# Probabilities and values of the last two units of self attention in fp32, weighted by single fp32 matmuls

## What is computed

```python
q = (x @ Wq.T + bq).reshape(B, T, N_HEADS, HEAD_DIM)
k = (x @ Wk.T + bk).reshape(B, T, N_KV_HEADS, HEAD_DIM)
v = (x @ Wv.T + bv).reshape(B, T, N_KV_HEADS, HEAD_DIM)
...
scores = jnp.einsum('bgkqd,bkld->bgkql', q, k) * SCALE
scores = jnp.where(causal, scores, jnp.float32(-jnp.inf))
w = jax.nn.softmax(scores, axis=-1)
out = jnp.einsum('bgkql,bkld->bgkqd', w, v)
```

## Time and profile before

| | |
|---|---|
| runs, us | 2606.54, 2605.93, 2609.09; median 2606.54 |
| profiled execution, us | 2608.02 |
| its span, us | 2606.2 |
| granted clock of TensorE, mean | 0.969 |
| busy: PE, DVE, ACT, POOL | 94%, 68%, 63%, 59% |

### The profile page before, as it was taken

How to read it: one execution, slowest core, us unless ns; L and a number is a source line. 1 busy time by engine, 2 the same in 40 slices (tenths; PEclk the granted TensorE clock), 3 DMA queues, 4 the chain that set the end, 5 groups by cost and what they waited for, 6 DMA issues and landing times.

```text
span 2606.2 us, 48453 instructions
## 1 busy us (share of the span) xinstructions
PE 2454.7 (94%) x17800; PEld 1350.7 (52%) x17800; DVE 1778.4 (68%) x2988; ACT 1638.7 (63%) x2998; POOL 1528.1 (59%) x1363
## 2 busy tenths in 40 slices
PE   7999999999986568999999999999999999999999
PEld 4667777777765453444444444444444444444444
DVE  6656777767777877777777777777777897645311
ACT  4556666666665447777777777777777786545100
POOL 2556677767778567777777777777766433212100
PEclk9999999999997679999999999999999999999999
DMA  6252433333322321222222222222223844323232
GB/s 218 89 160 89 125 123 121 113 107 102 92 86 82 96 73 41 89 90 89 86 85 86 86 84 91 89 90 92 87 84 106 262 138 150 107 90 106 70 109 76
DMA packets 224827, 271.09 MB, mean 104 GB/s; under 512 B 36560, under 2 KB 147664, under 8 KB 224592
## 3 DMA queue, kind: packets, MB, share of 16 engines
q1 hardware_dynamic: 224592, 268.00, 32.7%
HBM read 192.94 MB, written 73.40 MB: 102 GB/s over the span
## 4 chain that ended last, share of the span: by engine, by line
PE 54%; POOL 3%; issue 1%; DVE 1%; ACT 1%; DMA 0%; DVEq 0%; ACTq 0%; POOLq 0%
PE ps L2176 32%; PE ps L2209 22%; POOL q_rows L513 1%; POOL p L494 1%; POOL xn L2083 1%; POOL xT L483 0%; DMA h_parts<-xn 0%; DVE p L462 0%; DVE ps L462 0%; ACT q_rows L509 0%; POOL x_row L2089 0%; ACT w_l L452 0%; DVE xT L477 0%; ACT xn L2270 0%; ACT ps L449 0%
## 5 line engine op out<-in xcount | busy, mean ns | idle before, releaser
L462 DVE TENSOR_TENSOR ps<-ps,w_l 128x512 f32<-128x512 f32 x672 | 444.1, 693 | 242.8 <-ACT w_l L452 165.3
L1024 POOL TENSOR_TENSOR arena<-p,arena 128x512 f16<-128x512 f32 x320 | 370.8, 1167 | 227.6 <-ACT arena L1508 227.0
L483 POOL TENSOR_TENSOR xT<-xT,nat 128x512 f32<-128x512 f32 x162 | 206.4, 1274 | 451.9 <-DVE xT L477 451.9
L452 ACT ACTIVATE w_l<-proj 128x512 f32<-128x512 int32 x672 | 398.6, 617 | 60.9 <-DVE ps L462 51.7
L1500 ACT ACTIVATE p<-ps 128x512 f32<-128x512 f32 x320 | 191.1, 597 | 265.2 <-PE ps L1276 260.1
L1719 DVE TENSOR_REDUCE block_max<-ps 128x4 f32<-128x512 f32 x320 | 218.9, 687 | 176.0 <-PE ps L1247 173.4
L449 ACT ACTIVATE ps<-proj,small 128x512 f32<-128x512 int32 x336 | 217.7, 680 | 168.9 <-DVE xT L477 166.2
L2176 PE MATMUL ps<-arena,q_rows 128*128 128x512 f16 x1344 | 296.7, 380 | 5.4 <-DVE x_row L2356 3.8
L2436 DVE SCALAR_TENSOR_TENSOR arena<-ps,arena 128x1024 f32<-128x1024 f32 x70 | 85.2, 1220 | 211.5 <-PE ps L2209 208.8
L1217 PE MATMUL ps<-xT,w_h 128*128 128x512 f16 x720 | 218.4, 385 | 1.5 <-DVE xT L1673 1.5
L2176 PEld LDWEIGHTS ps<-arena,q_rows 128*128 128x128 f16 x1344 | 131.7, 98 | 166.0 <-issue 7.0
(11 more groups left out here) (253 smaller groups left out, 5941.7 us busy)
## 6 DMA issues: line engine op xcount, KB each, us to landing
proj<-in_codes SPq DMA_DIRECT2D x168, 256.0 KB, 2.9
nat<-in_scales SPq DMA_DIRECT2D x336, 128.0 KB, 2.9
h_parts<-xn SPq DMA_DIRECT2D x112, 256.0 KB, 2.4
nat_parts<-nat SPq DMA_DIRECT2D x48, 256.0 KB, 2.0
q_rows<-nat_parts SPq DMA_DIRECT2D x96, 128.0 KB, 2.8
w_l<-h_parts SPq DMA_DIRECT2D x21, 448.0 KB, 4.3
x_unit<-in_x SPq DMA_DIRECT2D x64, 128.0 KB, 2.7
x<-x_unit SPq DMA_DIRECT2D x64, 128.0 KB, 2.3
```

The lines of the kernel that those rows point to most:

```text
L452: op = self.nc.scalar.activation(out, self.t.codes[:, t % 2, :], ACT.Copy, scale=slope, bias=intercept)
L462: self.nc.vector.tensor_tensor(other if n == self.LUT - 2 else held, held, other, ALU.max).then_inc(self.lut, 1)
L483: self.nc.gpsimd.tensor_tensor(self.quarter(t), self.quarter(t), self.t.scales[:, t % 2, :], ALU.mult)\
L1024: nc.gpsimd.tensor_tensor(p_l[:, n % 2, k, :], p32[:, f % 3, :], p_h[:, n % 2, k, :], ALU.subtract).then_inc(p_low, 1)
```

## The change

For the pairs of the last two units (56 to 63, from `WIDE` on) the chunks aren't split. The exponential goes to one of thirteen fp32 buffers in turn: the three from before, and ten that lie over the buffers of the high and low halves, which these pairs don't use. The values of these units stay in fp32 as well, in a buffer that lies over that of their halves, with DVE writing the column of ones. `weigh_wide` waits for the pair's exponentials rather than low halves, and issues one fp32 matmul of 33 columns for each of the 20 blocks. The exponentials wait for a weighting (`o_done`) where they take a buffer that it reads. The statistics' small buffer `f_moments` and the buffers behind the values move by 16 words; at the start POOL clears the fp32 view of the values and writes the ones of the two halves' buffers in two instructions, so the waits on `selected` count one more. The diff, cut to its core:

```diff
-        arena = sb("arena", [P, 14360], FP32)
+        arena = sb("arena", [P, 14376], FP32)
...
-        self.v_parts = carve([P, 2, QT, PAIRS, 2 * D + 1], FP16)
+        values = carve([P, 2, QT * PAIRS * (D + 1)], FP32)
+        self.v32 = values.rearrange("p b (q j n) -> p b q j n", q=QT, j=PAIRS)
+        self.v_parts = [values[:, b, 0:QT * PAIRS * (2 * D + 1) // 2].bitcast(FP16)
+                        .rearrange("p (q j n) -> p q j n", q=QT, j=PAIRS) for b in range(2)]
...
+        self.p_wide = [buf[:].rearrange("p b k n -> p (b k n)").bitcast(FP32)[:, HALF * k:HALF * k + HALF]
+                       for buf in (self.p_h, self.p_l) for k in range(CHUNKS)]
...
+    WIDE = NS - 2 * PAIRS
+    RING = 3 + 2 * CHUNKS
...
+    def wide_p(f):
+        n = (f - CHUNKS * WIDE) % RING
+        return p32[:, (CHUNKS * WIDE + n) % 3, :] if n < 3 else t.p_wide[n - 3]
...
-                if 0 <= f < CHUNKS * NS:
+                if 0 <= f < CHUNKS * WIDE:
                     low_part(f)
...
-        cleared = [t.ident_b, t.mask_qk, t.mask_kq, t.v_parts, t.kx_h, t.kx_l, t.vx_h, t.vx_l]
+        cleared = [t.ident_b, t.mask_qk, t.mask_kq, t.v32, t.kx_h, t.kx_l, t.vx_h, t.vx_l]
...
-        nc.gpsimd.memset(t.v_parts[:, :, :, :, D:D + 1], 1.0).then_inc(selected, 1)
+        for b in range(2):
+            nc.gpsimd.memset(t.v_parts[b][:, :, :, D:D + 1], 1.0).then_inc(selected, 1)
...
+        def weigh_wide(n):
+            u, j = n // PAIRS, n % PAIRS
+            if j == 0:
+                pe.wait_ge(v_low, u + 1)
+            pe.wait_ge(t_exp, CHUNKS * (n + 1))
+            pe.wait_ge(max_out, min(n // 2 + (n % 2), NS // 2 - 1) + 1)
+            pe.wait_ge(o_read, n)
+            for qt in range(QT):
+                for hh in range(2):
+                    col = (D + 1) * (2 * qt + hh)
+                    for kt in range(qt + 1):
+                        k, at = t_place(hh, kt, qt)
+                        mm = nc.tensor.matmul(bank[O_BANK][:, col:col + D + 1], wide_p(CHUNKS * n + k)[:, at:at + P],
+                                              t.v32[:, u % 2, kt, j, :], start=(kt == 0), stop=(kt == qt))
+            mm.then_inc(o_done, 1)
...
-                    weigh(s - 1)
+                    (weigh if s - 1 < WIDE else weigh_wide)(s - 1)
...
-            nc.scalar.activation(t.v_parts[:, u % 2, :, :, 0:D],
+            values = t.v_parts[u % 2] if PAIRS * u < WIDE else t.v32[:, u % 2, :, :, :]
+            nc.scalar.activation(values[:, :, :, 0:D],
...
-            if f >= 3:
+            n = f - CHUNKS * WIDE
+            if 3 <= f and n < 3:
                 act.wait_ge(p_low, f - 2)
-            nc.scalar.activation(p32[:, f % 3, :], bank[T_BANK + T_OF[f % CHUNKS]][:, :], ACT.Exp,
+            elif n in (3, 3 + CHUNKS):
+                act.wait_ge(o_done, WIDE)
+            elif n >= RING:
+                act.wait_ge(o_done, WIDE + (n - RING) // CHUNKS + 1)
+            nc.scalar.activation(p32[:, f % 3, :] if n < 0 else wide_p(f), bank[T_BANK + T_OF[f % CHUNKS]][:, :], ACT.Exp,
                                  scale=SELF_SCALE).then_inc(t_exp, 1)
...
-                if k != 3 and 0 <= f - 1 < CHUNKS * NS:
+                if k != 3 and 0 <= f - 1 < CHUNKS * WIDE:
                     high_part(f - 1)
-                if k == 2 and 0 <= f < CHUNKS * NS:
+                if k == 2 and 0 <= f < CHUNKS * WIDE:
                     high_part(f)
...
             dve.wait_ge(v_high, u + 1)
+            if PAIRS * u >= WIDE:
+                nc.vector.memset(t.v32[:, u % 2, :, :, D:D + 1], 1.0).then_inc(v_low, 1)
+                return
```

More of the change, by code:

```diff
@@ L101, in __init__ @@
         self.bias_v = carve([P, KV * D], FP32)
-        self.vx_last = arena[:, 13336:13336 + KVX * 2 * (D + 1)].rearrange("p (g n) -> p g n", g=KVX)
-        self.px_last = self.v_parts[:].rearrange("p b q j n -> p (b q j n)")[:, 0:4 * HALF].bitcast(FP32) \
-            .rearrange("p (b n) -> p b n", b=2)
+        self.vx_last = arena[:, 13352:13352 + KVX * 2 * (D + 1)].rearrange("p (g n) -> p g n", g=KVX)
+        self.px_last = values.rearrange("p b n -> p (b n)")[:, 0:2 * HALF].rearrange("p (b n) -> p b n", b=2)
         self.f_stats = arena[:, 14336:14360].rearrange("p (w h n) -> p w h n", w=2, h=2)
+        self.f_moments = arena[:, 14360:14376].rearrange("p (b w n) -> p b w n", b=2, w=2)
         self.w_h = sb("w_h", [P, CT, 4 * HALF], FP16)
@@ L232, in __init__ @@
         self.stats = t.f_stats
-        moments = sb("f_moments", [P, 2, 2, 4], FP32)
+        moments = t.f_moments
         self.mean_var, self.var_eps, self.rstd = moments[:, :, :, 0:2], moments[:, :, :, 2], moments[:, :, :, 3]
@@ L1064, in step @@
             pair_lows(s, 0)
-            if 0 <= 5 * s < CHUNKS * NS:
+            if 0 <= 5 * s < CHUNKS * WIDE:
                 low_part(5 * s)
@@ L1112, in _ @@
                                 pattern=[[1, P]], channel_multiplier=-1).then_inc(selected, 1)
-        nc.gpsimd.memset(t.v_parts[:, :, :, :, D:D + 1], 1.0).then_inc(selected, 1)
-        pool.wait_ge(selected, 5)
+        for b in range(2):
+            nc.gpsimd.memset(t.v_parts[b][:, :, :, D:D + 1], 1.0).then_inc(selected, 1)
+        pool.wait_ge(selected, 6)
         nc.gpsimd.memset(t.k_rows[96:97, :, :, :], 1.0).then_inc(selected, 1)
         for j in range(2):
-            pool.wait_ge(selected, 6 + j)
+            pool.wait_ge(selected, 7 + j)
             nc.gpsimd.memset(t.vx_h[TC * j:TC * j + TC, :, (D + 1) * j + D:(D + 1) * j + D + 1], 1.0)\
                 .then_inc(selected, 1)
-        pool.wait_ge(selected, 8)
+        pool.wait_ge(selected, 9)
         for s in range(0, TO):
@@ L1294, in weigh @@
                         low = p_l[:, n % 2, k, at:at + P]
-                        v = t.v_parts[:, u % 2, kt, j, :]
+                        v = t.v_parts[u % 2][:, kt, j, :]
                         out = bank[O_BANK]
@@ L1424, in _ @@
             if s == -2:
-                pe.wait_ge(selected, 8)
+                pe.wait_ge(selected, 9)
             step(s)
@@ L1586, in _ @@
             if s == -2:
-                act.wait_ge(selected, 8)
+                act.wait_ge(selected, 9)
             step(s)
@@ L1712, in v_low_part @@
             dve.wait_ge(v_high, u + 1)
-            nc.vector.tensor_tensor(t.v_parts[:, u % 2, :, :, D + 1:2 * D + 1],
+            if PAIRS * u >= WIDE:
+                nc.vector.memset(t.v32[:, u % 2, :, :, D:D + 1], 1.0).then_inc(v_low, 1)
+                return
+            nc.vector.tensor_tensor(t.v_parts[u % 2][:, :, :, D + 1:2 * D + 1],
                                     proj32[:, 1, :].rearrange("p (q j d) -> p q j d", q=QT, d=D),
-                                    t.v_parts[:, u % 2, :, :, 0:D], ALU.subtract).then_inc(v_low, 1)
+                                    t.v_parts[u % 2][:, :, :, 0:D], ALU.subtract).then_inc(v_low, 1)
         def maximum(n, k):
@@ L1853, in _ @@
             if s == -1:
-                dve.wait_ge(selected, 8)
+                dve.wait_ge(selected, 9)
         for n in range(-2, NX + 4):
```

## The result

| | before | after |
|---|---|---|
| runs, us | 2606.54, 2605.93, 2609.09, 2604.30, 2609.46 | 2629.14, 2619.69, 2619.31, 2621.54, 2621.88 |
| median, us | 2606.54 | 2621.54 |
| profiled execution, us (its span) | 2608.02 (2606.2) | 2629.14 (2627.3) |
| mean granted clock in it | 0.969 | 0.962 |

The ratio is 1.0059, interval 1.0044 to 1.0074: **15.0 us slower** by the medians, inside the range, on the side that had 0.63. The profiled execution of after is the slowest of the five, so its trace shows 21 us in place of 15.

A forecast was written before the change was run, and what follows sets the result against it. It took a loop of TensorE, ACT, DVE and POOL, with no engine full, to bound the stretch. 31 us added less 15.4 and 6 made 10 us slower, 2616.5 us; range +5 to +20, 2611.5 to 2626.5.

The forecast's parts named there:

- the side that had 0.63: Whole kernel slower: chance 0.63, from 0.50 for +5 to +20 us and 0.13 for all weightings at half clock.
- Sum: 15.4 us earlier: Steps 57 to 64, weighting pairs 56 to 63: waits removed with the high and low halves, 15.4 us in all.
- Steps 61, 63 and 64: Waits before the weighting, for POOL, and behind ACT's halves go: 3.3, 3.2 and 2.5 us earlier.
- step 58: Wait of 2.14 us before the weighting goes and ACT's cross-attention high half comes earlier: 2.6 us together.
- step 59: Third of POOL's three waits, 0.5 us, and 0.2 of the earlier half: 0.7 us earlier.
- steps 60 and 62: Turned pair's copies, sum and second turn 1.1 us earlier; DVE's normalisation and copies freed of halves, 2.0 us.
- Two records each, distance set by the load: Each new fp32 matmul: two records, spaced by the weight load, 111 ns at full clock, 213 at half.
- The third rival: Columns set the record distance: 55 ns at full clock, kernel 6 us faster, 2600.5 us; chance 0.12.
- Added: 8 x (5.6 - 1.67) = 31 us: Eight fp32 weightings of 5.6 us at clock 0.78 replace fp16 ones of 1.67, adding 31 us on TensorE.
- What the longer weightings cover: TensorE's waits for DVE shrink: 5 us of block maxima and pair output, 1 after step 64, together 6.
- all at half clock: Rival: all weightings but the first at TensorE's lower clock, 27 us slower, 2633.5 us; chance 0.13.
- Full clock, not slower: Rival: longer weightings replace TensorE's waits and its clock stays 2.4 GHz, -3 to +2 us, 2605.5; chance 0.25.

The follow-up runs named there:

- the run without fp32: Changed kernel with exponentials in fp16, no halves, and each block weighted by three equal fp16 matmuls of 33 columns; 2594.32 us, 0.9960 of the kernel before.
- the repetition: The changed kernel measured again, unaltered, on another occasion; 2630.03 us, 1.0076 of the kernel before on the same chip.

## Why the prediction was right in direction and short in size

- **What goes away** ("Sum: 15.4 us earlier"): 12.2 by the run without fp32, and 4.5 of it came with a higher clock, which the sum did not have. Steps 61, 63 and 64 held within 0.4 us; step 58 gave 1.5 of 2.6, step 59 gave 2.6 for 0.7, so the total is closer than its items. What failed is where sums stand: steps 60 and 62 gave -0.7 and -0.5 for 1.1 and 2.0, because DVE was late next, in step 60 with a lower clock besides.
- **Two records each, distance set by the load**: right. 40 records per weighting, 112 and 213 ns, and the same with 17, 66 and 128 columns. The third rival (columns, 2600.5) is refuted twice: 17 columns gained nothing, 128 lost nothing. The four-pass rule of the Trainium skill ("FP8 and Floating Point Precision", "TensorE Precision Notes") that was named beside it does not price these matmuls: estimated from it, 17, 33 and 66 columns would be 28, 55 and 110 ns a matmul, and each took 222 to 224 at the full clock. At 128 columns it would be 213, which these runs can't tell from the two loads.
- **"Added: 8 x (5.6 - 1.67) = 31 us"**: mis-sized a little. The mean weighting was 5.94 us, so 34.2. The clock of these steps was taken from the trace of before (0.78), and it did not stay there. The Trainium skill's rule for the load ("TensorE: Matmul & The Clock Gate", "LDWEIGHTS (loading the stationary operand)"), with no term for the clock, would make 4.3 us of each; the last two took 8.50 and 8.53 at the half clock, so here too the measurement decides against it.
- **What the longer weightings cover** (6, beside the 15.4): right. TensorE's idle time fell by 20.9 us, 21.4 had been written down. The waits for block maxima and the pair's output went from 7.0 to 2.5, so 4.5 for the 5. The waits for sums, which I had called not covered, halved, but they do so without the longer weightings too (5.7). Behind the last weighting TensorE's idle time fell by 1.2 for the 1 (7.21 to 5.97), though its other work there took 0.85 longer: that step grew by 6.4 us for a weighting 6.8 longer.
- **What was left out**: TensorE's other work. The sum charged the half clock to the weightings alone; the same instructions around them took 7.7 us longer in the profiled run, since the clock fell within the weightings and stayed low behind them. This is the step that failed: 9.6 (31 - 15.4 - 6) + 7.7 + 3.2 (34.2 in place of 31) + 0.5 (20.9 in place of 21.4) = 21.0, as in the profile. The median run lost 15, so a run in the middle has about half of this surplus; the repetition lost 23.5 against before on its chip. That the first measurement lies inside the +5 to +20 is thus partly luck: the mechanism that was priced is there, and the term that was left out can carry a run past the end of the range.
- **Where it shows**: "steps 57 to 59 longer, 61 to 64 about as long as now" is wrong for the second half. By step the stretch grew by 2.2, 3.3, 0.4, 0.1, 1.9, 2.0, 4.7 and 6.4 us: 15.0 of 21 in the last four, where the clock is 0.63, 0.74, 0.59 and 0.50. The rest from there to the end is as before, as said.
- **The other rivals**: all at half clock came for two weightings of eight, for three in the repetition's profile. Full clock, not slower, priced at -3 to +2 us (2605.5), is about what 128 columns make true: 2604.0, 3.3 below before on its chip, with a clock (0.91) near its condition of 0.95. Its reason for doubt, that the clock is low in these steps now, pointed the right way for another cause: with the same loads and the same order, 33 columns in place of 128 take the clock from 0.91 to 0.67.
- **A misreading without effect**: TensorE is 57 to 85% busy in the earlier trace rows (7.30 of 12.70 is the least), not 66 to 85; no term of the sum uses it.

## What to carry to other kernels

When a change puts different matmuls in TensorE's order, price the instructions around them at the clock that the new ones leave, not at the clock of the old trace: here that was worth more than the mis-sizing of the matmuls themselves. An fp32 matmul with 128 weight columns cost two records of 111 ns at the full clock with anything from 17 to 128 columns, so fewer columns saved nothing, and a stream of 128 columns was 0.7 to 0.9% faster than one of 33 (ratios to before of 0.9985, and of 1.0059 and 1.0076). And a removed wait is worth what the next engine in the loop leaves of it: 12 of 15 us here, and 4.5 of the 12 came with a higher clock.

## What the runs showed of the hardware that was not expected

- TensorE's granted clock falls to its lower level within a run of fp32 matmuls of 33 columns without a gap among them: the scores behind the first weighting take 0.61 us and six cross-attention matmuls 1.48, against 0.38 and 0.82 behind one of 128 columns, within which the clock rose from the half to the full level. A TensorE busy 85% of the stretch had 0.67, one busy 63% had 0.77 before.
- With 17, 33, 66 and 128 columns the record distance stays at 111 to 112 ns (213 at the half clock).
- Single runs of one kernel differ by what the clock does: the kernel with only the last unit in fp32 had runs from 2601.92 to 2626.08 us, that with 128 columns from 2599.68 to 2605.61. The kernel before scatters too (2598.44 to 2617.79 in 21 runs on the chip of the first of these), so one profile of such a kernel stands for one run.
